# A gated int8 layer and a routed MoE on one core: weight splits moved into the first stage, two base products ahead of the first gather, small maxima in PSUM, layer norms on VectorE

## What is computed

```python
x = x + tanh(g_xattn) * xattn(layernorm(x), fside, ctx)      # 4 x (256 x 256)
x = x + tanh(g_ffn) * ffn(layernorm(x), ...)                 # 1024 tokens of 256
# xattn, per batch: two linear layers with int8 rounding (SmoothQuant)
#   s = sqrt(max|x| / max|w|) per column;  xs = x / s;  ws = w * s
#   round(xs / (max|xs| / 127)) @ round(ws / (max|ws| / 127)).T, scaled back; silu(gate) * up between
# ffn: conf = sigmoid(x @ conf_W.T + conf_b) * wealth; the best 2 of 8 experts per token
#   g = x @ base_gate + x @ gate_A[e] @ gate_B[e] / 4            (256 -> 896; rank 64)
#   u = x @ base_up   + x @ up_A[e]   @ up_B[e]   / 4
#   h = silu(g) * u;  out += share * (h @ base_down + h @ down_A[e] @ down_B[e] / 4)
```

## Time and profile before

| what | value |
|---|---|
| median of three runs | 347.58 us |
| the profiled execution, its own time | 349.11 us |
| its span, first to last instruction | 347.2 us |
| PE busy | 261.5 us (75%) |
| DVE busy | 201.3 us (58%) |
| ACT busy | 167.1 us (48%) |
| POOL busy | 133.8 us (39%) |

### The profile page before, as it was taken

One profiled execution on the slowest core, in us unless ns is written; L12 is line 12 of the kernel. 1 busy time (PEld: TensorE's weight loads), 2 busy tenths in 40 slices (PEclk: granted clock), 3 DMA queues, 4 the chain that ended last, 5 costly groups with the idle time before them and its releaser, 6 DMA issues.

```text
span 347.2 us, 5197 instructions
## 1 busy us (share of the span) xinstructions
PE 261.5 (75%) x1540; PEld 236.1 (68%) x1541; DVE 201.3 (58%) x409; ACT 167.1 (48%) x285; POOL 133.8 (39%) x162
## 2 busy tenths in 40 slices
PE   2569547988981003995999999999999999997700
PEld 1446435877971002994999999999999999996600
DVE  4598997661497000016667767777777677776115
ACT  2448875756354351253555545555555555555011
POOL 5396614220057995018233333333333333311111
PEclk9855997899996555898999999999999999999755
DMA  8545210025348674226244444444444444400065
GB/s 255 166 124 124 62 31 30 32 106 206 161 154 248 189 206 127 105 120 217 83 135 146 139 130 137 142 138 139 143 141 135 144 137 138 145 21 15 17 205 173
DMA packets 30190, 45.69 MB, mean 132 GB/s; under 512 B 13976, under 2 KB 25632, under 8 KB 30176
## 3 DMA queue, kind: packets, MB, share of 16 engines
q0 software_dynamic: 4416, 21.50, 18.7%
q1 hardware_dynamic: 21840, 14.55, 14.8%
q10 hardware_dynamic: 3920, 9.46, 7.2%
HBM read 33.57 MB, written 11.93 MB: 131 GB/s over the span
## 4 chain that ended last, share of the span: by engine, by line
PE 62%; DVE 10%; DMA 10%; POOL 6%; ACT 6%; issue 3%; SPq 2%; ACTq 0%; DVEq 0%
PE pY L55 8%; PE pY L59 7%; PE pY L57 7%; PE pG L55 5%; PE pT L1548 4%; PE pG L57 4%; PE pG L59 4%; PE pU L57 3%; PE pU L59 3%; PE pU L55 3%; DMA q<-in_ctx_dram 3%; PE bank L1254 2%; DMA yr<-results 2%; DMA raw<-in_L_ffn_down_A_dram 2%; POOL WdA_lo L440 2%
## 5 line engine op out<-in xcount | busy, mean ns | idle before, releaser
L525 POOL DMA_INDIRECT results<-yb,dest x19 | 18.8, 987 | 94.4 <-DVE yb L1188 94.4
L55 PE MATMUL pY<-Wd_hi,hT_hi 128*128 128x384 f32 x133 | 48.3, 363 | 1.1 <-ACT Wd_lo L789 0.8
L59 PE MATMUL pY<-Wd_hi,hT_lo 128*128 128x384 f32 x133 | 45.3, 341 | 0.0
L57 PE MATMUL pY<-Wd_lo,hT_hi 128*128 128x384 f32 x133 | 45.3, 341 | 0.0
L519 POOL DMA_INDIRECT bin<-base_products,tok x18 | 22.0, 1220 | 26.9 <-PE pU L59 17.1
L799 ACT CAST hT_hi<-pT 128x896 fp32r<-128x896 f32 x19 | 17.2, 907 | 24.1 <-PE pT L1548 24.1
L1511 PE MATMUL pX<-ident,xin 128*128 128x128 f32 x38 | 7.5, 280 | 27.9 <-DMA xin<-normed,tok 27.9
L55 PEld LDWEIGHTS pY<-Wd_hi,hT_hi 128*128 128x128 f32 x133 | 25.4, 191 | 3.3 <-issue 1.0
L775 ACT CAST xaT_hi<-pX 128x256 fp32r<-128x256 f32 x19 | 7.1, 374 | 42.5 <-PE pX L1525 42.1
L1118 DVE TENSOR_TENSOR xT_lo<-pX,xT_hi 128x256 fp32r<-128x256 f32 x19 | 7.9, 416 | 31.0 <-ACT xT_hi L769 31.0
L57 PEld LDWEIGHTS pY<-Wd_lo,hT_hi 128*128 128x128 f32 x133 | 25.6, 193 | 0.0
(11 more groups left out here) (234 smaller groups left out, 778.4 us busy)
## 6 DMA issues: line engine op xcount, KB each, us to landing
base_products<-brow ACTq DMA_DIRECT2D x8, 896.0 KB, 3.6
yr<-results SPq DMA_DIRECT2D x8, 256.0 KB, 5.4
raw<-in_L_ffn_down_A_dram SPq DMA_DIRECT2D x7, 256.0 KB, 3.0
raw<-in_L_ffn_gate_B_dram SPq DMA_DIRECT2D x8, 224.0 KB, 2.8
raw<-in_L_ffn_up_B_dram SPq DMA_DIRECT2D x8, 224.0 KB, 2.8
x_resid<-in_x_dram SPq DMA_DIRECT2D x4, 256.0 KB, 5.1
q<-in_fside_BxS2xS_dram ACTq DMA_DIRECT2D x4, 256.0 KB, 5.7
normed<-q ACTq DMA_DIRECT2D x4, 256.0 KB, 2.2
```

Source lines behind the costliest of these rows:

```text
L55: m.matmul(outs[i], hi, whi[i], start=first, stop=False, skip_group_check=True)
L57: m.matmul(outs[i], hi, wlo[i], start=False, stop=False, skip_group_check=True)
L59: ins = m.matmul(outs[i], lo, whi[i], start=False, stop=last, skip_group_check=True)
L525: g.indirect_dma_start(out=yg, out_offset=bass.IndirectOffsetOnAxis(ap=dest[:, j:j + 1], axis=0), in_=yb[:, :], in_offset=None).then_inc(d ...
```

## The change

1. `RING` goes from 4 to 6.
2. The splits of the 25 later chunks are spread over the lists of ACT and POOL: on POOL 12 of them stand between `roots2(1)` and `deviations2(3)`, the other 13 behind `deviations2(3)`; on ACT they stand in ones, twos and threes from `integers_w(2)` on, the last ahead of `s_plan`.
3. `normal1` and `normal2` go from ACT to DVE: (x - mean) * rstd in one tensor_scalar per tile, L900. POOL's product `nmr` is gone (two small instructions per batch and norm). DVE adds the epsilon by a tensor_reduce over a column that holds it (L886), so that POOL reads `spread`.
4. `ratio`'s four small operations become two (L915, L916; L948, L949 for the gated rows). The reciprocals are taken ahead, in `weights_amax` (two more operations) and in `context_amax` (two more). The maxima lie in unused columns of `alpha(b)` and `beta(b)`, in PSUM, also those that `scales` reads.
5. On PE `base(4)`, `base(5)` and `base_half(6, 0)` stand between ranks and sort, `base_half(6, 1)` and `base(7)` behind the sort, ahead of `x_T(0)`; ACT copies tiles 6 and 7 ahead of its wait for the plan. `direct(0)` and `direct(1)` (tile 0's own products) stand around `xa_T(0)`.
6. On DVE `stats2(1)` is ahead of `x2_lo(0)`.

```diff
-        RING, RW = 4, 512
+        RING, RW = 6, 512
...
-            def deviations(b, source, made, root, rooted, product, done_):
+            def deviations(b, wide, made, root, rooted):
...
-                g.tensor_tensor(root[:, ts], source[:, ts, 1], half[:, 0, 0:TB], ALU.pow).then_inc(rooted, 1)
-                pool.wait_ge(rooted, b + 1)
-                for t in range(TB * b, TB * (b + 1)):
-                    ins = g.tensor_scalar(product[:, t:t + 1], source[:, t, 0:1], root[:, t:t + 1], -1.0, ALU.mult, ALU.mult)
-                ins.then_inc(done_, 1)
+                g.tensor_tensor(root[:, ts], wide[:, ts], half[:, 0, 0:TB], ALU.pow).then_inc(rooted, 1)
...
             roots2(1)
+            lo(4)
             gated(2)
             deviations2(0)
+            lo(1)
             roots2(2)
+            lo(1)
             gated(3)
             deviations2(1)
+            lo(1)
             roots2(3)
+            lo(4)
             deviations2(2)
+            lo(1)
             deviations2(3)
             lo(CH_1 - lo_done[0])
...
             act.wait_ge(s_rounder, 2)
-            normal1(0)
             split(2)
-            normal1(1)
             split(6)
-            normal1(2)
             weights_scaled(0)
...
             integers_w(2)
-            split(1)
+            split(3)
             scaled2(0)
             scales_w(2)
             integers2(0)
+            split(1)
             scales_c(0)
+            split(1)
...
             scales_c(1)
-            normal2(0)
+            split(1)
             scales_w(3)
             x2_hi(0)
+            split(1)
             silu1(3)
+            split(2)
             conf_rows(0)
-            normal2(1)
...
             integers2(2)
+            split(1)
...
             integers2(3)
+            split(1)
             base_half(1, 0)
             scales_c(3)
-            normal2(2)
+            split(1)
             base_half(1, 1)
             base_store(1)
+            split(1)
             x2_hi(2)
-            normal2(3)
...
             conf_rows(3)
+            split(1)
             act.wait_ge(s_logit, 1)
             a.activation(bids[:, :, :], bids[:, :, :], ACT.Sigmoid).then_inc(s_sig, 1)
+            split(2)
             base_half(3, 0)
+            split(1)
             base_half(3, 1)
             base_store(3)
+            split(2)
             base_half(4, 0)
...
+            split(2)
             base_half(4, 1)
             base_store(4)
             split(2)
...
             base_store(5)
-            split(2)
             split(CH_1)
-
+            for t in range(PRE, NT):
+                base_out(t)
 
             act.wait_ge(s_plan, 1)
...
             x_hi(0)
-            for t in range(PRE, NT):
-                base_out(t)
             xa_hi(0, first=True)
...
+                c = beta(b)[:, S + 8:S + 9]
+                link(v.tensor_reduce(c, beta(b)[:, 0:S], AX_X, ALU.max, apply_absolute_value=True))
+                link(v.tensor_scalar(c, c, EPS, None, ALU.max))
+                v.reciprocal(rcp_c[:, b:b + 1], c).then_inc(s_camax, 1)
...
+            def normal(b, moments, root, rooted, made):
+                dve.wait_ge(rooted, b + 1)
+                for j in range(TB):
+                    t = TB * b + j
+                    ins = v.tensor_scalar(q1[:, j, b, :], xs_all[:, t, :], moments[:, t, 0:1], root[:, t:t + 1], ALU.subtract, ALU.mult)
+                ins.then_inc(made, 1)
...
-                ratio(amx[:, b, 0, :], amx[:, b, 1, :], amx[:, b], tmp8[:, b, :], s_ratio)
+                link(v.scalar_tensor_tensor(out=x_, in0=x_, scalar=EPS, in1=rcp_w[:, b, :], op0=ALU.max, op1=ALU.mult))
+                v.tensor_scalar(tmp8[:, b, :], x_, EPS * EPS, None, ALU.max).then_inc(s_ratio, 1)
...
-                link(v.tensor_reduce(am1[:, b, :], q1[:, :, b, :], AX_X, ALU.max, apply_absolute_value=True))
-                scales(am1[:, b, :], inv1[:, b, :], sc1[:, b, :], s_inv1)
+                am = beta(b)[:, 0:4]
+                link(v.tensor_reduce(am, q1[:, :, b, :], AX_X, ALU.max, apply_absolute_value=True))
+                scales(am, inv1[:, b, :], sc1[:, b, :], s_inv1)
...
             rows_amax(1)
+            normal1(2)
             smooth1(0)
...
             dequantise1(3)
+            stats2(1)
             x2_lo(0)
-            stats2(1)
+            normal2(1)
...
             base_half(3, 0)
             base_half(3, 1)
-            base_half(4, 0)
 
             pe.wait_ge(s_pickb, 1)
...
             ins.then_inc(s_rank, 1)
-            base_half(4, 1)
-            base_half(5, 0)
-            base_half(5, 1)
+            base(4)
+            base(5)
+            base_half(6, 0)
...
             ins.then_inc(s_sorted, 1)
+            base_half(6, 1)
+            base(7)
...
             x_T(0)
-            base(PRE)
             pe.wait_ge(s_wlo, CH_A)
             project_A(0, group(0))
-            base(PRE + 1)
+            direct(0)
             xa_T(0)
...
+            direct(1).then_inc(s_direct, 1)
```

More of the change, by code:

```diff
@@ L424, in _ @@
                 g.memset(rounder[:, i:i + 1], value).then_inc(s_rounder, 1)
+            g.memset(amx_w[:, :, :, 1], EPS).then_inc(s_eps, 1)
+            for moments in (mv, mv2):
+                g.memset(moments[:, :, 2], LN_EPS).then_inc(s_eps, 1)
             for i, value in enumerate((-0.5, 0.5)):
@@ L582, in _ @@
             done = [0]
-            def normal(b, ready, root, shift, made):
-                act.wait_ge(ready, b + 1)
-                for j in range(TB):
-                    t = TB * b + j
-                    ins = a.activation(q1[:, j, b, :], xs_all[:, t, :], ACT.Identity, scale=root[:, t:t + 1], bias=shift[:, t:t + 1])
-                ins.then_inc(made, 1)
-            def normal1(b):
-                normal(b, s_nmr, rstd, nmr, s_xn)
-            def normal2(b):
-                normal(b, s_nmr2, rstd2, nmr2, s_x2)
             def rows_scaled(b):
@@ L887, in stats1 @@
                 dve.wait_ge(d_x[b], 16)
-                statistics(b, bst, mv, s_var)
+                statistics(b, bst, mv, spread, s_var)
             def stats2(b):
                 dve.wait_ge(s_x1, b + 1)
-                statistics(b, bst2, mv2, s_var2)
-            def ratio(of, over, clamped, to, made):
-                link(v.tensor_scalar(clamped, clamped, EPS, None, ALU.max))
-                link(v.reciprocal(to, over))
-                link(v.tensor_tensor(to, of, to, ALU.mult))
-                v.tensor_scalar(to, to, EPS * EPS, None, ALU.max).then_inc(made, 1)
+                statistics(b, bst2, mv2, spread2, s_var2)
@@ L1597, in tile, with direct @@
                 h_T(j)
+            def direct(gu):
+                pe.wait_ge((s_bgc, s_buc)[gu], NT)
+                for c in range(HC):
+                    ins = base_product((pG, pU)[gu], gu, c, xT_hi[:, c, :], xT_lo[:, c, :], False)
+                return ins
             x_T(0)
[L1600 removed]
             pe.wait_ge(s_wlo, CH_A)
             project_A(0, group(0))
[L1603 removed]
+            direct(0)
             xa_T(0)
[L1606 to L1610 removed]
+            direct(1).then_inc(s_direct, 1)
             pe.wait_ge(s_xalo, 1)
```

75 lines of the change are left out of this document (43 added, 32 removed).

## The result

The changed kernel takes 320.59 us (median of 4 runs, 318.96 to 322.74), the kernel before 347.2 (median of 4, 346.81 to 350.02): a ratio of 0.9221, with a 95% interval of 0.9138 to 0.9305. A second comparison, made with the experiments, gave 320.40 and 0.9239 (0.9204 to 0.9275). The forecast was 321.4 us, in a range of 314 to 329. The profiled execution took 319.21 us with a span of 317.5, against 349.11 and 347.2 before. So the two profiled executions differ by 29.9 us and the medians by 26.6; a difference of 1 or 2 us between two profiles is not a finding.

The account below looks back on a forecast made before the run. POOL's 25 splits held the gather 22.4 us past its data, and PE made base products late. 33.2 - 1.5 - 4.5 - 1.0 = 26.2 us gained from a median of 347.58 gave 321.4 us, range 314 to 329.

Parts of the forecast that it names:

- Splits and base products, 33.2: On PE up to the second transpose of gathered rows: `x_T(1)` at 121.1 in place of 154.30, 33.2 us gained.
- rival (b): POOL's last 13 splits late for the gather, so `x_T(0)` waits 7.1 us longer: time 328.5 us; chance 0.11.
- the rest of 193 us: PE from `x_T(1)` to the end: the program is as before, 192.9 us taken as unchanged.
- First stage, -1.5: DVE and POOL lists grow by 4.4 us; a third reaches the stage's end, +1.5 us, bounds -4 to +8.
- The excess of the small operations on SBUF: First stage, DVE: small operations slowed where POOL splits; moving maxima to PSUM takes away 5.0 us.
- The norms: First stage, DVE: six of eight meet a busy DVE, 4.2 us at 0.35 each, plus 4.5 waiting for splits.
- The table load: First stage, ACT: 1.28 us now ahead of the first split, so POOL's first three splits come 1.3 us later.
- The picks, -4.5: DVE's expert picks beside five POOL splits: 5.4 us of waiting, so PE's ranks lose 4.5 us.
- Clock, -1.0: PE slower after its pause ahead of the ranks: 1.0 us lost, of 0 to 2.
- rival (c): PE's clock stays low in the eight halves; two halves cost 4.6 us: time 325.0 us; chance 0.10.
- The cover of the gather, 1.9 us to spare: Ahead of `x_T(0)`: gathered rows arrive at 111.6, hidden under PE's three halves with 1.9 us of cover.
- (a): POOL and DVE miss one another and the first stage comes out even: time 314.4 us; chance 0.16.

Follow-up runs that it names:

- none at all: Changed kernel with the last 13 splits moved from beside the picks and the plan to behind the gather, on POOL and ACT: 318.70 us, ratio 0.9171.
- the splits on ACT sooner: Changed kernel with the last 13 splits behind the gather, an earlier sort on PE, and ACT's seven late splits moved forward: 316.12 us, ratio 0.9111.

## Why the prediction was right, step by step

The sum was 33.2 - 1.5 - 4.5 - 1.0 = 26.2 us; the profiled executions have `x_T(1)` 28.9 us earlier, and the medians differ by 26.6. The mechanism was right, three of the four terms were off in size. That the median came within 0.8 us of the forecast is in part luck: the sum is 2.7 us short of what the profiled execution gained at `x_T(1)`, but that execution lies 1.4 us under the median of its kernel, and the profiled one before 1.9 over the median of its own.

- **Splits and base products, 33.2.** Right: the losses found below (0.3, 1.7 + 0.2, 0.7 and 1.6, so 4.5 us) and the 28.9 gained make 33.4. The sign that the prediction named for rival (b), `x_T(0)` waiting for `xin`, did appear, with 0.70 us; but POOL had been idle for 2.83 us when the gather started, and what it waited for was DVE. So the rival's cause did not come, and the rest of 193 us stayed (192.1). The losses are the stage, the waits for `pickb` and `attrib`, the one for `xin` and the low clock. The experiments add what the sum did not say, that the two edits need one another: the base copies on ACT stand behind the splits.
- **First stage, -1.5.** It was -0.3 (-1.0 in the second execution, within the scatter). The excess of the small operations on SBUF went (5.0 us counted; 5.3 found when the maxima were put back). The norms met fewer splits than I had counted: two pairs took 1.45 and 1.67 us instead of 0.73, so 1.7 us and not 4.5, and an unhindered norm took 0.41 us (0.73 the pair), near the 0.35 taken. The table load stood where I had put it, but POOL's first split came only 0.6 us later than before (15.20 for 14.59) and not 1.3, and the run with the load moved away shows nothing of it at the stage's end. The step that failed is how I weighed it: I added the terms up and let a third through, where the runs show that the splits without norms and maxima cost 5.3 to 6.0 us and that norms and maxima pay back nearly all of that.
- **The picks, -4.5.** The wait was 1.71 us. Four operations were stretched, by 2.5 us together, half a split each on average, and `pickb` came 2.7 us late (93.67 for 90.93); I had counted nearly all five splits at their full length. Of these five, one started behind `pickb`, and DVE went on with other operations while the others ran.
- **Clock, -1.0.** PE's wait ahead of the ranks, 1.71 us, slowed nothing. But behind the wait of 1.49 us for `xT_lo` six matmuls took 0.41 us where they take 0.28 in the run with splits alone, and three pairs 0.95, 0.95 and 0.79 for 0.57: 1.6 us, counted from start to start. The busy time by stretch shows both places, with the granted clock in the third column from the end:

```profile
92.00:107.00 15.00, 13.29 (x93) 12.00 (x92) 13.69 (x30) 9.23 (x16) 10.54 (x9) 1.00 0.68 233
116.08:125.41 9.33, 7.84 (x34) 7.01 (x35) 1.27 (x3) 2.47 (x5) 0.94 (x1) 0.82 0.30 112
```

  From 92 to 107 us, the ranks and the halves behind them, PE was granted the full 2.4 GHz; behind `x_T(0)` the mean is 0.82, and from 117.98 to 121.54 alone 0.52, the lower level. The size was near, the place wrong. Counted from start to start, a slow pair takes 0.75 us for 0.41, so it costs 0.34; the prediction's 0.38 came from durations that overlap. Its 2.3 us for six pairs is 2.0, and the 4.6 of rival (c) is 4.1.
- **The cover of the gather, 1.9 us to spare.** It was missing by 0.70, so 2.6 us were left out. `tok` came not 2.1 but 3.0 us behind the sort's end, since DVE was still at L1113 and L1116 (1.16 and 0.77 us) beside POOL's last splits; from `tok` to the gather, where I had nothing, there are 1.05 (one more operation of DVE and 0.9 from its end to POOL's start); and from the gather to its use it took 4.0, not 3.4. 0.9 + 1.05 + 0.65 = 2.6.

Of the rivals, (a) stated the price of meetings: 4.5 and more. With none at all the gain was 1.9 us of the median, as other waits took their place. (c), a slow clock for two halves, was priced at 4.6; the same mechanism cost 1.6. The errors cancelled in part: 3.8 us too much for the picks (2.6) and the stage (1.2), 1.3 too little for the gather's cover (0.7) and the clock (0.6).

## What to carry to other kernels

When an in-order engine does background work ahead of a critical instruction, first look for who else stands behind that work: here it was PE, by way of ACT's copies, so that two reorderings gained 23.0 us together and 17.7 one by one. An edit that makes room (small operations to PSUM, norms to another engine) showed nearly nothing at the stage's end when it stood alone and 5.7 us beside the splits that fill the room; test such a part with and without what fills the room, not only alone. And after each fix read the plan's own waits again: the order that suits a slow plan (the sort behind five halves) was what held the fast one, and setting it right may have brought as much again (2.2 us by the medians, whose intervals overlap; with the splits on ACT sooner, the gain over the changed kernel is shown).
